# A feed-forward kernel behind a long convolution: K sums moved to the prologue, one turn of q given to a transfer, and the moves around them

## What is computed

```
K    = 2 * real(einsum('hn,hnl->hl', Cs, exp(dtA * arange(512))))
y    = (irfft(rfft(x * mask) * rfft(K)) + x * mask * D) * mask
yq   = int4_quant(y)                     # one scale for each row, values -8 to 7
gate = yq @ quant(w_gate).T ;  up = yq @ quant(w_up).T      # 512 -> 1376
inter= int8_quant(up * relu(gate)**2)
out  = x + inter @ quant(w_down).T                          # 1376 -> 512
```

## Time and profile before

| | |
|---|---|
| runs of the kernel | 205.87, 205.91, 206.24 us |
| the profiled execution, its own time | 205.13 us |
| its span | 203.0 us |
| busy, share of the span | PE 86%, DVE 82%, ACT 56%, POOL 6% |
| mean granted clock of PE | 0.992 of full |

### The profile page before, as it was taken

How to read it: one execution, slowest core, us unless ns; L and a number is a source line. 1 busy time by engine, 2 the same in 40 slices (tenths; PEclk the granted TensorE clock), 3 DMA queues, 4 the chain that set the end, 5 groups by cost and what they waited for, 6 DMA issues and landing times.

```text
span 203.0 us, 3423 instructions
## 1 busy us (share of the span) xinstructions
PE 174.0 (86%) x1127; PEld 93.7 (46%) x1143; DVE 166.2 (82%) x456; ACT 114.2 (56%) x188; POOL 11.7 (6%) x31
## 2 busy tenths in 40 slices
PE   1001699899899999999999999999999999998883
PEld 1001696554545454545454545454544454443352
DVE  6999888779997698888888878787878797978871
ACT  2186986799717282819191918182727364644730
POOL 8122500100001000000000000000000000000000
PEclk9999969999999999999999999999999999999999
DMA  2999939376898376756666665659565687245504
GB/s 84 371 385 338 316 103 332 124 247 124 164 187 174 138 152 204 151 164 143 176 133 185 134 182 135 184 129 183 132 182 149 157 137 181 67 96 56 116 6 103
DMA packets 48224, 34.12 MB, mean 168 GB/s; under 512 B 36512, under 2 KB 36880, under 8 KB 48208
## 3 DMA queue, kind: packets, MB, share of 16 engines
q1 hardware_dynamic: 47408, 32.38, 64.1%
q10 hardware_dynamic: 416, 1.47, 2.0%
q0 software_dynamic: 384, 0.06, 0.3%
HBM read 21.07 MB, written 4.28 MB: 125 GB/s over the span
## 4 chain that ended last, share of the span: by engine, by line
PE 70%; DVE 12%; DMA 7%; ACT 7%; issue 3%; SPq 0%; DVEq 0%; ACTq 0%
PE conv_ps L508 16%; PE gate_ps L591 15%; PE down_ps L641 15%; PE up_ps L596 14%; PE tr_act_ps L498 3%; DMA q_int<-y_i 2%; DMA toep<-k_back 2%; DMA k_back<-k_sb 2%; ACT g L749 1%; ACT int_gate L692 1%; ACT int_down L685 1%; DVE inter L1107 1%; PE tr_dve_ps L641 1%; PE up_ps L544 1%; PE tr_dve_ps L565 1%
## 5 line engine op out<-in xcount | busy, mean ns | idle before, releaser
L596 PE MATMUL up_ps<-up_t,q_t 128*128 128x416 bf16 (+2 forms) x192 | 45.0, 357 | 0.0
L707 ACT ACTIVATE y_abs<-y 128x512 bf16<-128x512 f32 x16 | 10.1, 629 | 61.1 <-DVE y L1022 61.1
L591 PE MATMUL gate_ps<-gate_t,q_t 128*128 128x416 bf16 (+2 forms) x177 | 41.9, 356 | 2.4 <-DVE q_t L1042 1.5
L1107 DVE SCALAR_TENSOR_TENSOR inter<-up_ps,gu_scale,g 128x416 f32<-128x416 f32 (+2 forms) x48 | 33.2, 692 | 6.8 <-issue 4.6
L508 PE MATMUL conv_ps<-toep,x_t 128*64 128x512 f32 (+3 forms) x256 | 38.0, 439 | 0.7 <-DMA toep<-k_back 0.5
L641 PE MATMUL down_ps<-down_t,i_t 128*128 128x512 bf16 (+1 forms) x153 | 35.3, 379 | 1.2 <-DVE i_t L1146 1.2
L749 ACT ACTIVATE g<-gate_ps,gu_scale 128x416 f32<-128x416 f32 (+2 forms) x48 | 30.3, 631 | 6.1 <-PE gate_ps L591 6.1
L1111 DVE TENSOR_REDUCE imax<-inter 128x1 f32<-128x416 f32 (+2 forms) x48 | 30.3, 631 | 1.6
L752 ACT ACTIVATE g<-g 128x416 f32<-128x416 f32 (+2 forms) x48 | 28.1, 585 | 1.5
L508 PEld LDWEIGHTS conv_ps<-toep,x_t 128*64 128x64 f32 x256 | 17.2, 136 | 23.5 <-issue 20.5
L596 PEld LDWEIGHTS up_ps<-up_t,q_t 128*128 128x128 bf16 x192 | 18.8, 98 | 18.4
(11 more groups left out here) (186 smaller groups left out, 170.9 us busy)
## 6 DMA issues: line engine op xcount, KB each, us to landing
toep<-k_back SPq DMA_DIRECT2D x16, 512.0 KB, 4.0
out_dram<-o_sb SPq DMA_DIRECT2D x30, 128.0 KB, 2.4
x_in<-in_x_dram SPq DMA_DIRECT2D x24, 128.0 KB, 3.1
raw_gate<-in_L_ffn_w_gate_dram SPq DMA_DIRECT2D x1, 1536.0 KB, 7.0
raw_up<-in_L_ffn_w_up_dram SPq DMA_DIRECT2D x1, 1536.0 KB, 13.5
raw_down<-in_L_ffn_w_down_dram ACTq DMA_DIRECT2D x1, 1376.0 KB, 6.9
raw_down<-in_L_ffn_w_down_dram SPq DMA_DIRECT2D x1, 1376.0 KB, 10.8
raw_gate<-in_L_ffn_w_gate_dram SPq DMA_DIRECT2D x1, 1024.0 KB, 9.3
```

Source lines behind the costliest of these rows:

```text
L591: mm = pe.matmul(gate_ps[bank][:, 0:cn], q_t[p][:, i, :], gate_t[:, i, c0:c0 + cn], start=(i == 0), stop=(i == KB - 1))
L596: mm = pe.matmul(up_ps[bank][:, 0:cn], q_t[p][:, i, :], up_t[:, i, c0:c0 + cn], start=(i == 0), stop=(i == KB - 1))
L1107: v.scalar_tensor_tensor(out=inter[:, c0:c0 + cn], in0=up_ps[bank][:, 0:cn], scalar=gu_scale[p][:, 1:2], in1=g2[bank][:, 0:cn], op0=ALU.mu ...
```

## The change

- `Q_BY_DMA` goes from 3 to 2: q of tile 2 is turned by a transfer on SP's queue, not by PE. In SP's iteration 1 that transfer stands ahead of `turn_down(0)`, which moves behind it. On DVE `q_copy(2)` moves from behind `gated(2)` to behind `gated(1)` of iteration 1, ahead of the cast of `i_t`.
- `k_sums(3)` leaves PE's iteration 1. Four of its eight heads (`K_CUT` is 12) are summed in the prologue behind `k_sums(1)`, with a wait for the mean of w_up, whose sum lies in the same bank; the other four stand behind `qt(0)`.
- `xt(0)` moves ahead of `mean(1)` on PE.
- `load_x(1)` moves on SP's queue from ahead of the store of K part 0 to behind `load_toep(0)`.
- `xt_copy(3)` (ACT) moves ahead of `relu_square(2)` of iteration 1.
- `q_copy(0)` moves ahead of `k_copy(2)` on DVE.

```diff
-        Q_BY_DMA = 3
+        Q_BY_DMA = 2
+        K_CUT = 3 * HG // 4
@@ SP, prologue
             load_x(0)
-            load_x(1)
...
             load_toep(0, 0)
+            load_x(1)
             load_toep(1, 1)
@@ SP, body
-                if k == 1:
-                    turn_down(0)
...
                     sp.dma_start_transpose(q_int[:], y_i[:]).then_inc(q_loaded, 16)
+                if k == 1:
+                    turn_down(0)
@@ PE, prologue
-            def k_sums(i):
+            def k_sums(i, first=0, last=HG):
...
-                for h in range(h0, h1):
+                for h in range(max(h0, first), min(h1, last)):
...
-                mm.then_inc(k_summed, 1)
+                if last >= h1:
+                    mm.then_inc(k_summed, 1)
...
             k_sums(0)
+            xt(0, 0, 0)
             mean(1)
-            xt(0, 0, 0)
             pe.wait_ge(tables_ready, 2)
             k_sums(1)
+            pe.wait_ge(winv_ready, 2)
+            k_sums(3, last=K_CUT)
...
             qt(0)
+            k_sums(3, first=K_CUT)
@@ PE, body
-                if k == 1:
-                    k_sums(3)
@@ ACT, body
                 if k == 1:
                     y_round(2)
+                    xt_copy(3)
...
-                elif k < T - 2:
+                elif 2 <= k < T - 2:
                     xt_copy(m + 2)
@@ DVE
             weight_copy(10)
+            q_copy(0, 0)
             k_copy(2)
-            q_copy(0, 0)
@@ DVE, body (behind gated(1), ahead of the cast of i_t)
+                if k == 1:
+                    q_copy(2, 0)
...
-                if 1 <= k < T - 1:
+                if 2 <= k < T - 1:
                     q_copy(m + 1, 1 - p)
```

## The result

The changed kernel takes 207.82 us (median of four runs, 207.69 to 208.85), the kernel before 206.01 beside it: a ratio of 1.009 with a 95% interval of 1.0052 to 1.0128. It is slower by 1.8 us. The profiled execution took 207.69 us with a span of 205.6.

What follows compares the result with a forecast made beforehand. PE, busy 86%, was taken as the bound, with DVE's slack only 0.57 us in iteration 1. Terms -0.17 + 1.17 = +1.0 us on the median 205.91 gave 206.9; forecast's own range 206.5 to 207.5, whole range 205.3 to 208.2.

Steps and rivals of the forecast that it cites:

- PE's gain of 1.13 in iteration 1: Iteration 1: convolution of tile 3 starts at 55.15, not 56.28, as turn and K sums leave PE.
- the signs that were to make the prediction wrong: PE wait under 1.1 before first down product; front >0.4 earlier at 48; clock 0.50 after 55; new PE gap behind 66.
- Front, -0.17: Front, products of tile 0: q copied ahead of K starts them 0.17 us sooner; ends -0.7 and +0.6.
- First down product, +1.17: Iteration 1, PE's first down product: w_down's last turn lands at 61.9 after 4.4 us, copy ends 62.85, start +1.17 us.
- rival A: Iteration 1: turns land by 61.3, DVE alone decides first down product, +0.57; +0.4 in all, 206.3; chance 22%.
- Second down product, +0 with 0.5 at the high end: Iteration 1, second down product: inter_q's turn of tile 1 starts at 62.0, lands 65.6 to 66.5; nothing added, 0.5 high end.
- B: Iteration 1: instruction fetch meets q's turn at 56 to 57, DVE waits 1.9 more; +2.3, 208.2; 17% together with C.
- C: Iteration 1: PE's clock falls for some 3 us behind gaps of 1.1 and 2.3; +2.5, 208.4; 17% together with B.
- D: Front gains more than iteration 1 loses if tile 0's convolution starts before 30.9; -0.6, 205.3, extreme -1.3, 204.6; chance 19%.

Runs made afterwards that it cites:

- experiment 3: Changed kernel with q of tile 2 turned by PE again, w_down's turn in its old place, q_copy behind gated(2): 205.4 us, ratio 0.9979.
- experiment 6: Kernel before with the q part alone: q of tile 2 by transfer ahead of w_down's first turn, q_copy ahead of the cast: 208.6 us.
- the repeat: The changed kernel itself run and profiled once more, nothing altered: 208.3 us, ratio 1.0097 to the kernel before.
- experiment 4: Changed kernel with x and Toeplitz form of tile 4 issued ahead of the turn of q: 209.0 us, ratio 1.0142.
- experiment 5: Changed kernel with x and Toeplitz form of tile 4 issued ahead of the turn of inter_q of tile 0: 209.3 us, ratio 1.0166.
- experiment 9: Changed kernel with x and Toeplitz form of tile 4 issued behind the turn of inter_q of tile 1: 208.3 us, ratio 1.0112.
- experiment 1: Changed kernel with x of tile 1 loaded ahead of the K store again: 207.9 us, ratio 1.0088.
- experiment 7: Changed kernel with q_copy of tile 2 on DVE behind gated(2) again: 208.3 us, ratio 1.0121.
- experiment 2: Kernel before with x of tile 1 alone moved behind the first Toeplitz load: 205.9 us, ratio 0.9987.
- experiment 8: Changed kernel with q of tile 2 on PE, but q_copy(2) kept early, ahead of the cast: 205.3 us, ratio 0.9970.
- experiment 10: As experiment 8, with the front moves undone (x of tile 1, x turn of tile 0, K copy order): 206.0 us, ratio 0.9993.

## Why the prediction was right, and where its sum was off

**Direction and mechanism.** The prediction said that PE's gain of 1.13 in iteration 1 turns into a wait for DVE's copy of w_down, because q by transfer comes late for DVE and pushes w_down's turns back on SP. The trace shows most of it: PE began the convolution of tile 3 8.67 us after that of tile 2 in place of 9.80, the 1.13 predicted; q landed 2.3 us after its issue, DVE was idle for 0.97 (1.06 predicted), and PE waited 1.49. Experiments 3 and 6 show that this part alone is the loss. One link was not as predicted: the copy of w_down did not wait for the turns. And of the signs that were to make the prediction wrong, one came true: a new gap of PE behind 66, the 1.50 ahead of 68.84. The mechanism that was predicted is in the trace, but it is the smaller part of the loss, 0.5 of the 2.2 us lost in iteration 1.

**Front, -0.17.** In the profile after no wait stands ahead of 38.92, where there had been 0.75 ahead of 38.32, as predicted. From the convolution of tile 0 to that of tile 2, the stretch in which this wait lies, it is 47.08 - 32.51 = 14.57 us in place of 46.48 - 31.68 = 14.80: -0.23. The repeat has 14.72. How much sooner or later the convolution of tile 0 itself starts can't be read from two profiles: it waits for the Toeplitz load, which landed after 3.8 to 5.2 us in the kernels that have x of tile 1 behind it. From the medians the front would be what iteration 1 leaves over: 1.8 of loss against 2.2 in iteration 1 (21.76 against 19.58), so about -0.4. But the same subtraction gives -0.7 for the sixth kernel, whose front is that of the kernel before (2.6 against 3.3), so it carries no term of this size.

**First down product, +1.17.** Measured +0.52 (15.77 against 15.25), and +0.64 in the repeat. The step that was off is the landing of w_down's second turn: I took 4.4 us, and it took 3.8 and was there when DVE came to it at 61.82. So rival A's +0.57, DVE alone, was what happened.

**Second down product, +0 with 0.5 at the high end.** This is the term that was wrong. Measured 68.84 - 62.85 = 5.99 us from the first to the second, against 66.06 - 61.73 = 4.33: +1.66. I had seen that the turn of inter_q of tile 1 would be issued at 62.0 (61.88 measured) and gave it 3.6 to 4.5 us to land. It took 6.4. Where the loads of tile 4 are not ahead of it (experiments 4, 5 and 9) it took 3.5; where they are, but were issued 1.1 us and more ahead of it, as in the kernel before, 4.3 to 4.5. So the moment of issue was right, and the time to landing that I took for it was not: it left out the loads that would stand 0.7 us ahead. I had put extra time on w_down's turns instead, because two of them had taken over 5 us, and a fetch stood beside those two.

**Sum.** +1.0 was predicted and +1.8 measured. Iteration 1 alone has +0.52 + 1.66 = +2.2; the -0.4 that is left over is in no term that a trace shows. The first term was too large by 0.65 and the second too small by 1.66, so part of the nearness is luck: 207.8 lies above the forecast's own 206.5 to 207.5, in the part of the range that was there for the rivals B and C, neither of which happened. (Two thirds of A's 22% are 15, not 16; nothing hangs on it.)

**The rivals.** B, a turn of q hit on its way, did not happen in the changed kernel (2.3 and 2.4 us, the second with a fetch at the moment of its issue). In experiment 6 it took 3.6 beside a fetch, and the first down product came 1.3 later than expected, but in four other runs a fetch that close cost the turn at most 0.3. So the price is not settled, and the fetch as the cause rests on a coincidence in time. The rule of the Trainium skill that it was weighed against (DMA: Bandwidth & Descriptors, Queues, rings and completion order), transfer engines alternating between queues packet by packet, does not by itself give the 3.25 of the row at 65.0, where q8 has no fetch; what does is open. C, the fall of the clock, did not happen in the changed kernel and did in the fourth, behind the longest gap. TensorE: Matmul & The Clock Gate of the Trainium skill, under HAM oscillation, names waits for transfers between stretches of matmuls as what brings the clock down; the 2.91 us of the fourth, a wait for DVE that itself waited for q's transfer, agree, while 2.08 us of the same wait in the fifth brought no fall. The gap of 1.67 that I had taken as agreeing was a wait for ACT. D falls: the first convolution started at 32.51, not before 30.9.

## What to carry to other kernels

A step given from PE to a transfer is not free because PE waits elsewhere: ask which engine waits for its result in order, and what stands behind it on the issuing queue. Follow the queue until the next transfer that somebody needs, not only to the one that was moved. Here the costly one had five other transfers between itself and the one that was moved. Counted from the convolution of tile 2 it was issued 1.55 us later than before (61.88 - 47.08 against 59.73 - 46.48), and took 1.9 longer to land (6.4 against 4.5); both had to be in the sum.

## What the runs showed of the hardware

- In iterations 1 and 2, turns by transfer with no plain load ahead in the queue landed after 3.5 to 4.0 us (inter_q), 2.3 to 2.6 (q of tile 2; 3.6 once, in experiment 6) and 3.7 to 3.8 (w_down in the changed kernel).
- With 0.75 MB of plain loads ahead, the last of them issued 0.6 to 0.7 us before the turn, they took 6.2 to 6.7 (inter_q, in the changed kernel, its repeat, and experiments 1, 5, 6 and 7) and 4.8 to 5.1 (q, in 9 and 4; 4.6 in 5, with one turn between). With the last of the loads issued 1.1 to 2.0 us before it, inter_q's took 4.3 to 4.5 (the kernel before, experiments 2, 3, 8 and 10).
- w_down's last two turns took 5.2 to 5.7 in the four kernels in which an instruction fetch on q8 fell into their time (the one before, 2, 3 and 8), and 3.7 and 4.0 in experiment 10, in which it fell earlier.
- The granted clock of PE fell to 0.50 with a gap of 2.91 us (experiment 4) and stayed at 1.00 after one of 2.08 (experiment 5), each behind 2.4 us of work that had itself followed a gap of 1.1. At the start of the kernel before it fell at 26.5, behind a gap of only 1.67. So the length of the last gap alone does not tell.
- The same Toeplitz load of 0.5 MB at the front of the changed kernel landed after 5.1 us in one execution and 3.8 in the repeat, and 32 K sums took 1.11 us in the one and 29 of them 1.73 in the other. The front differs by tenths from one execution to the next.
